# A tuned attention kernel: the last unit gets an order of its own, and GpSimd prepares two of the closing tiles

## The reference, cut to what matters

```python
xn = _layernorm(x)                                   # x: 8 x 256 x 512
q, k, v = heads of xn @ wq.T, xn @ wk.T, xn @ wv.T   # 32 query heads, 8 key/value heads of 128
q, k = rope(q), rope(k)
scores = (q @ k.T) / sqrt(128) * scale + causal      # scale: 0.5 or 1.5 on some columns
s = softmax(scores) @ v, all heads side by side, @ wo.T
g = silu(lora_mixture(xn))                           # top 2 of 4 experts
out = x + s * g
```

## Time and profile before

| | us |
|---|---|
| median of 3 runs | 1355.3 (1354.82 to 1359.77) |
| the profiled execution, its own time | 1357.92 |
| its span, first to last instruction | 1356.1 |
| PE busy | 1322.2 (98%) |
| DVE busy | 969.6 (72%) |
| ACT busy | 961.8 (71%) |
| POOL busy | 423.0 (31%) |
| granted TensorE clock, mean | 0.99 |

### The profile page before, as it was taken

One profiled execution on the slowest core, in us unless ns is written; L12 is line 12 of the kernel. 1 busy time (PEld: TensorE's weight loads), 2 busy tenths in 40 slices (PEclk: granted clock), 3 DMA queues, 4 the chain that ended last, 5 costly groups with the idle time before them and its releaser, 6 DMA issues.

```text
span 1356.1 us, 22594 instructions
## 1 busy us (share of the span) xinstructions
PE 1322.2 (98%) x6982; PEld 1106.6 (82%) x6982; DVE 969.6 (72%) x2449; ACT 961.8 (71%) x2513; POOL 423.0 (31%) x341
## 2 busy tenths in 40 slices
PE   7599999999999999999999999999999999999997
PEld 5588888788888888888888888888888888888885
DVE  6786678667766777776776777677777767777775
ACT  3586668777777777687776768777676877777773
POOL 4332321403314142143323224141331433223321
PEclk9699999999999999999999999999999999999998
DMA  6000000201100000010000000000000100012223
GB/s 217 16 17 5 24 24 9 62 17 47 47 24 32 0 23 23 0 31 15 23 8 15 15 15 31 0 31 0 23 23 0 31 15 23 8 31 85 73 80 119
DMA packets 23385, 43.64 MB, mean 32 GB/s; under 512 B 2480, under 2 KB 2608, under 8 KB 23344
## 3 DMA queue, kind: packets, MB, share of 16 engines
q1 hardware_dynamic: 20592, 37.76, 9.0%
q10 hardware_dynamic: 2752, 5.38, 1.1%
HBM read 34.74 MB, written 8.39 MB: 32 GB/s over the span
## 4 chain that ended last, share of the span: by engine, by line
PE 93%; DVE 4%; ACT 1%; issue 1%; DMA 1%; POOL 0%; SPq 0%; ACTq 0%; DVEq 0%
PE bank_a L461 19%; PE bank_b L461 18%; PE bank_b L555 13%; PE o_ps L555 12%; PE pv_ps L548 10%; PE pair L532 7%; PE pair L539 6%; PE pair L528 2%; PE pair L530 1%; PE bank_a L518 1%; PE o_ps L461 1%; DVE x_sb L975 1%; PE o_ps L508 1%; DMA x_sb<-x 1%; DVE pT_lo L1117 0%
## 5 line engine op out<-in xcount | busy, mean ns | idle before, releaser
L376 POOL TENSOR_TENSOR rot<-rot,tab 128x512 f32<-128x512 f32 x160 | 208.3, 1304 | 603.2 <-ACT rot L777 602.9
L820 ACT ACTIVATE probs<-probs,row_min 128x128 f32<-128x128 f32 (+1 forms) x512 | 225.5, 447 | 0.0
L839 ACT ACTIVATE pT_hi<-pair 128x768 fp32r<-128x768 f32 x128 | 104.0, 812 | 170.9 <-PE pair L539 170.2
L831 ACT ACTIVATE probs<-probs,row_inv 128x128 f32<-128x128 f32 (+1 forms) x512 | 190.8, 446 | 26.7 <-DVE row_inv L1147 26.4
L1117 DVE TENSOR_TENSOR pT_lo<-pair,pT_hi 128x768 fp32r<-128x768 f32 x128 | 121.7, 950 | 92.6 <-ACT pT_hi L839 92.3
L361 POOL TENSOR_TENSOR w_hi<-raw,zero 128x512 fp32r<-128x512 f32 x74 | 84.8, 1147 | 247.6 <-PE bank_a L461 131.2
L461 PE MATMUL bank_b<-xT_hi,w_hi 128*128 (+1 forms) x380 | 153.3, 403 | 2.8 <-DVE xT_lo L988 2.8
L461 PE MATMUL bank_a<-xT_hi,w_hi 128*128 (+1 forms) x380 | 154.8, 408 | 0.5 <-DVE xT_lo L988 0.4
L1097 DVE TENSOR_TENSOR q_lo<-cosx,q_hi 128x512 fp32r<-128x512 f32 x128 | 118.2, 924 | 47.1 <-ACT q_hi L784 46.9
L461 PE MATMUL bank_b<-xT_hi,w_lo 128*128 (+1 forms) x380 | 149.5, 393 | 0.0
L461 PE MATMUL bank_b<-xT_lo,w_hi 128*128 (+1 forms) x380 | 149.1, 392 | 0.0
(11 more groups left out here) (166 smaller groups left out, 3237.6 us busy)
## 6 DMA issues: line engine op xcount, KB each, us to landing
raw<-w_seq SPq DMA_DIRECT2D x76, 256.0 KB, 2.6
gate_scratch<-b_raw ACTq DMA_DIRECT2D x16, 256.0 KB, 2.0
out<-y_sum SPq DMA_DIRECT2D x16, 256.0 KB, 2.0
x_sb<-x SPq DMA_DIRECT2D x3, 1024.0 KB, 12.6
mid<-x SPq DMA_DIRECT2D x8, 256.0 KB, 2.7
mid<-gate_scratch SPq DMA_DIRECT2D x8, 256.0 KB, 2.9
raw<-x SPq DMA_DIRECT2D x7, 256.0 KB, 2.7
raw<-gate_scratch SPq DMA_DIRECT2D x7, 256.0 KB, 2.9
```

Source lines behind the costliest of these rows:

```text
L376: nc.gpsimd.tensor_tensor(v, v, tab[:, s:s + SEQ].unsqueeze(1).to_broadcast([P, 2, SEQ]), ALU.mult).then_inc(sin_done[kind], 1)
L820: a = nc.scalar.activation(s, s, ACT.Exp, bias=row_min[:, j % 2, i:i + 1], scale=-1.0, accum_out=row_sum[:, i:i + 1])
L831: a = nc.scalar.activation(s, s, ACT.Copy, scale=row_inv[:, i:i + 1])
L839: nc.scalar.activation(pT_hi[:, :, :], pair[j % 2][:, :, 0:ROWS], ACT.Copy).then_inc(pThi_done, 1)
```

## The change

The last unit is written out for itself on PE, ACT and DVE (`pe_closing`, `act_closing`, `dve_closing`). On PE an output tile stands behind each `turn_probs`, where the turned pair is being split. On ACT `low_scores(2)` goes ahead of `normalise_rows(1)`, and `exponents(3)` ahead of `rows_high(2)`. On DVE the tile additions move behind the steps of the items. For tiles 14 and 15 GpSimd first turns `y` into `x + y * gate`. DVE then multiplies the last unit's part by the gate and adds it: two operations after the matmuls in place of three. A fourth place for x and gate, `v_T` and `k_full`, takes tile 14. SP loads tiles 15 and 14 after tile 11, and tiles 12 and 13 after the stores of 10 and 11.

```diff
@@ sp
-            loop(sp, 0, TILES // 2 - 2, two_tiles)
+            loop(sp, 0, TILES // 2 - 3, two_tiles)
             sp.wait_ge(q_ready[H2], UNITS)
             load_xg(TILES - 1, 2)
-            store_tile(TILES - 4)
-            load_xg(TILES - 2, 0)
-            for t in range(TILES - 3, TILES):
+            sp.wait_ge(q_ready[K], UNITS)
+            sp.wait_ge(vt_ps, UNITS)
+            load_xg(TILES - 2, 3)
+            for s in range(2):
+                store_tile(TILES - 6 + s)
+                load_xg(TILES - 4 + s, s)
+            for t in range(TILES - 4, TILES):
                 store_tile(t)
@@ gpsimd
+            def open_tile(t, s):
+                y = y_sum[:, t, :]
+                pool.wait_ge(xg_in[s], 32)
+                pool.wait_ge(y_added, 4 * UNITS - 2 * TILES + t + 1)
+                nc.gpsimd.tensor_tensor(y, y, xg[s][1], ALU.mult).then_inc(base_scaled, 1)
+                pool.wait_ge(base_scaled, t - TILES + 3)
+                nc.gpsimd.tensor_tensor(y, y, xg[s][0], ALU.add).then_inc(base_done, 1)
+            def pool_closing():
+                open_tile(TILES - 2, 3)
+                add_residual(TILES - 4, 0)
+                add_residual(TILES - 3, 1)
+                open_tile(TILES - 1, 2)
@@ tensor
+        def pe_closing():
+            pe = nc.tensor
+            n = 4 * UNITS
+            pe.wait_ge(probs_ready, n - 3)
+            turn_probs(0)
+            output_tile(1, 0, n - 4, n - 7)
+            next_scores(2, n - 3, (), None)
+            pe.wait_ge(v_ready, UNITS)
+            prob_value(0)
+            pe.wait_ge(probs_ready, n - 2)
+            turn_probs(1)
+            output_tile(1, 1, n - 4, n - 6)
+            next_scores(3, n - 2, (), None)
+            pe.wait_ge(attn_ready, n - 3)
+            prob_value(1)
+            pe.wait_ge(probs_ready, n - 1)
+            turn_probs(2)
+            output_tile(0, 0, n - 2, n - 5, weights=KV_HEADS)
+            pe.wait_ge(pT_ready, n - 1)
+            prob_value(2)
+            pe.wait_ge(probs_ready, n)
+            turn_probs(3)
+            output_tile(0, 1, n - 2, n - 4)
+            pe.wait_ge(attn_ready, n - 1)
+            output_heads(1, 0, pair[0][:, 0, :], range(0, 2))
+            pe.wait_ge(pT_ready, n)
+            prob_value(3)
+            output_heads(1, 1, pair[0][:, 1, :], range(0, 2))
+            pe.wait_ge(attn_ready, n)
+            for t in range(2):
+                output_heads(1, t, pair[0][:, t, :], range(2, GROUP)).then_inc(o_done, 1)
@@ scalar
+        def act_closing():
+            rows_high(0, 125, 124)
+            low_scores(2, 127)
+            normalise_rows(1, 126)
+            rows_high(1, 126, 125)
+            attn_high(0, 125, 122)
+            exponents(2, 127)
+            low_scores(3, 128)
+            normalise_rows(2, 127)
+            attn_high(1, 126, 122)
+            exponents(3, 128)
+            rows_high(2, 127, 126)
+            normalise_rows(3, 128)
+            rows_high(3, 128, 127)
+            attn_high(2, 127, 124)
+            attn_high(3, 128, 124)
@@ vector
+        def close_tile(t, done, s):
+            dve, i = nc.vector, t - TILES + 2
+            dve.wait_ge(base_done, i + 1)
+            dve.wait_ge(o_done, done)
+            nc.vector.tensor_tensor(xg[s][1], pair[0][:, i, :], xg[s][1], ALU.mult).then_inc(o_gated, 1)
+            dve.wait_ge(o_gated, i + 1)
+            dve.wait_ge(y_final, t)
+            nc.vector.tensor_tensor(y_sum[:, t, :], y_sum[:, t, :], xg[s][1], ALU.add).then_inc(y_final, 1)
+        def dve_closing():
+            rows_low(0, 125)
+            mask_rows(2, 127)
+            rows_low(1, 126)
+            add_tile(10, 123, final=10, bank=o_ps[:, :], xg_set=0)
+            attn_low(0, 125)
+            row_inverse(127)
+            mask_rows(3, 128)
+            attn_low(1, 126)
+            add_tile(11, 124, final=11, bank=bank_b[:, :], xg_set=1)
+            row_inverse(128)
+            rows_low(2, 127)
+            add_tile(12, 125, final=12, bank=o_ps[:, :], xg_set=0)
+            rows_low(3, 128)
+            attn_low(2, 127)
+            add_tile(13, 126, final=13, bank=bank_b[:, :], xg_set=1)
+            attn_low(3, 128)
+            close_tile(14, 127, 3)
+            close_tile(15, 128, 2)
```

## The result

The changed kernel takes 1350.98 us (median of 6 runs) against 1356.72 for the kernel before in the same runs: ratio 0.9959, 95% interval 0.9946 to 0.9973. One of its six executions was a slow one (2181.95 us, mean granted clock 0.557), and the ratio goes by the other five, 1350.82 to 1351.34. The kernel is faster by 0.41%. The prediction took anything within 0.5% for "same", to which it gave 0.60, and the time lies inside its range of 1346.5 to 1352.0. The profiled execution took 1350.96, its span is 1349.0.

What follows compares the result with a forecast made beforehand. TensorE, busy 98% of the span, was taken as the bound, so its waits and slow clock near the end and the VectorE close count. The laid-out queues gave 6.8 off 1355.3, less 0.2: 1348.7, range 1346.5 to 1352.0.

Steps and rivals of the forecast that it cites:

- Step 1: ScalarE's normalise_rows(1) now stands behind low_scores(2), so turn_probs(1) starts at 1323.2 after a new TensorE wait of 0.8.
- Step 2: Tile 11 runs while the turned pair 1 is split, so the 1.89 wait before scores(3) is gone.
- Step 3: prob_value(1) follows scores(3) to 1328.9; the attn_low(0) it needs ends on VectorE at 1327.84, just in time.
- Step 4: turn_probs(2) waits 0.8 for normalise_rows(2); tile 12 starts 0.35 late, its attn_low(1) being behind mask_rows(3).
- Step 5: Tile 12 covers the old 2.58 wait before prob_value(2); rows_low(2) ends at 1333.95 with nothing to spare.
- Steps 6 and 7: TensorE's last tiles run to 1345.44, four closing VectorE operations instead of six end at 1346.90; span 1349.3, 6.8 less.
- The 0.2 for leaks: Allowance taken off the 6.8 because steps 3, 5 and 6 have 0 to 0.2 to spare, leaving 6.6.
- GpSimd and DMA: Prepared tile 15 ready 1.4 ahead, loads hidden with 0.5 for tile 13; only tile 12's multiply meets GpSimd, for 0.1 to 0.2.
- clock rival: The old slow clock is part of the gain, or the new queues slow once: gain 5.1 or 5.3, 1350.2 or 1350.0; chance 0.20.
- Close late: GpSimd's tile 15 or the load of 13 comes late, giving 1 to 3 back: 1350 to 1352; chance 0.07.
- Waits only move: Each TensorE wait taken away comes back behind ScalarE: 1 to 2 us and the shorter VectorE end remain, 1352 to 1354; 0.05.
- Slower: The new waits drop TensorE's clock to 0.50 from 1323 to the end: slower by 13, 1368; chance 0.04.

Runs made afterwards that it cites:

- The repeat: The changed kernel run again with no edit: closing stretch (last unit's first turn of probabilities to span's end) 32.97 us, median 1352.22 against 1357.99 for the kernel before.
- Experiment 8: The changed kernel with normalise_rows(1) ahead of low_scores(2) on ScalarE: closing stretch 31.91, ratio 0.9946 to the kernel before.
- Experiment 6: The changed kernel with tile 11's matmuls put back ahead of turn_probs(1): closing stretch 35.06, ratio 0.9968 to the kernel before.
- Experiment 5: The changed kernel with tile 12's matmuls put back behind turn_probs(3): closing stretch 37.76, ratio 0.9995 to the kernel before.
- experiment 3: The changed kernel's orders and loads alone, GpSimd preparing nothing, three closing operations each for tiles 14 and 15: closing stretch 34.29, ratio 0.9964 to the kernel before.
- prepared tiles alone: The last unit in the old order, but tiles 14 and 15 prepared by GpSimd and closed with two operations: closing stretch 38.59, ratio 0.9994 to the kernel before.
- experiment 2: The kernel before with useless matmuls filling its two TensorE waits in the last unit: closing stretch 38.00, ratio 0.9982 to the unfilled kernel.
- experiment 7: The changed kernel with GpSimd's two prepared tiles both after adding x to tiles 12 and 13: closing stretch 34.35, ratio 0.9960 to the kernel before.
- split tiles: The changed kernel with normalise_rows(1) first, tiles 12 and 13 halved, VectorE's additions of tiles 10 and 11 earlier: closing stretch 31.97, ratio 0.9942 to the kernel before.

## Why the prediction was right

- **What bounds it, and the sum.** 6.8 was worked out for the closing stretch, 6.62 measured. The repeat is 6.55 under the same profile of before.
- **Step 1**, new wait of 0.8 before `turn_probs(1)`: measured 0.80. Experiment 8 shows that it is paid in full (1.0 with the handover).
- **Step 2**, the 1.89 gone by tile 11's cover: right. Experiment 6 brings it back.
- **Step 3**, just in time: `prob_value(1)` started with no wait listed.
- **Step 4**, 0.8 and 0.35: measured 0.66 and 0.33.
- **Step 5**, the 2.58 gone: right. Experiment 5 shows tile 12 as the cover, which alone is worth 4.9, clock included. "Nothing to spare" held: `prob_value(2)` starts at 1333.48, `rows_low(2)` ends at 1333.42.
- **Steps 6 and 7**: from tile 14's last half (1342.04) to the last VectorE operation's end (1346.59) 4.55 passed, 4.38 were worked out. Four closing operations in place of six are worth 1.39 (experiment 3).
- **The 0.2 for leaks.** 6.8 less 0.2 is 6.6, and 6.62 came, but the 0.2 was taken for steps 3, 5 and 6, and these leaked nothing. Counted from the first turn, TensorE starts every step within 0.07 of the layout, and the last 12 matmuls at 25.94 in both. The 0.18 is lost in step 7. From the start of those 12 matmuls to VectorE's first closing operation the layout has 1.58, as before. The changed kernel took 1.76, in both of its profiles, "order alone" 1.70, "prepared tiles alone" 1.64. So 0.12 comes with the new order: the last 12 matmuls start as `attn_low(3)` ends, and the second follows the first by 0.34, not 0.23. And 0.06 comes with the two-operation close, for which no run shows a reason. The size of the allowance was right, its place was luck. The lines are of the kernel before, of "order alone" and of "prepared tiles alone":

```profile
1347.91 0.39 PE L555 MATMUL pair<-w_hi,attn_hi 128*128 128x512 f32 x1
```
```profile
1343.84 0.50 PE L577 MATMUL pair<-w_hi,attn_hi 128*128 128x512 f32 x1
1345.54 0.69 DVE L1322 TENSOR_TENSOR y_sum<-pair,y_sum 128x512 f32<-128x512 f32 x1 [1.75 <-PE pair L577]
```
```profile
1349.25 0.39 PE L579 MATMUL pair<-w_hi,attn_hi 128*128 128x512 f32 x1
```

- **GpSimd and DMA.** GpSimd was through 1.5 before it was needed, 1.4 forecast. The sign of the one meeting was the wrong way round: tile 12's multiply (1334.36, 0.69) started almost at GpSimd's end, and it was GpSimd's next addition that took 1.64. Both are hidden. I took 4.1 as the slowest landing; with the added loads behind one another it was 5.3, and it did no harm, since the data of `k_full` was there at 1327.7 and wanted at 1333.17, that of `cosx` much later. The loads of 12 and 13 had more room than the 0.5 forecast for tile 13: they landed some 2.1 before their multiplies. The two slowest loads:

```profile
cosx<-gate_scratch SPq DMA_DIRECT2D x1, 256.0 KB, 4.9
...
k_full<-gate_scratch SPq DMA_DIRECT2D x1, 256.0 KB, 5.3
```

- **The clock.** Counted as 1.7 of the gain, 1.5 by experiment 2. That the new waits would leave it at 1.00 held in all windows of the changed kernel from 1316 to 1346.
- **The signs.** Of the three signs of being wrong that were named, two did not come: a clock of 0.50 after 1323, and a wait before `prob_value(2)`. The third did: the stretch before 1316 changed its length. The last unit began 0.48 earlier than in the profile of before, and 0.75 later in the repeat. That sign was badly chosen, since this start moves between executions of one program; the closing stretch leaves it out.
- **The absolute time.** 1348.7 forecast, 1350.98 measured. 1.4 of these 2.3 is the kernel before, whose median was 1355.3 in the runs shown and 1356.72 over all. With 6.6 off that it would be 1350.1, and the rest, 0.9, is inside the interval of the ratio (1349.4 to 1353.1 from 1356.72). The start of the last unit varies by 3.4 between profiles of identical instructions, so a gain of 6.6 does not show sharper than this in a few runs. The time alone would not have carried the forecast. 1350.98 lies above the forecast's own 1347.0 to 1349.6, 0.8 over the clock rival's 1350.2 and among the late close's 1350 to 1352; it is the closing stretch that decides between them. And the repeat's median of 1352.22, with the same gain (0.9951), lies above the range's top of 1352.0. That the first one fell inside was in part luck.
- **The rivals.** "Close late" was made real by experiment 7: it costs 1.45, within its 1 to 3. "The clock gives less" had no case in these profiles: the clock was down in the one of before, and filling the waits gave 1.5. "Waits only move" happened to the small part that steps 1 and 4 say. "Slower" had nothing for it.

That part of the gain depends on where the clock falls in other executions of the kernel before stays open: only one of its executions was traced.

## What to carry to other kernels

Lay out an in-order schedule by hand before trusting a reordering: durations of one trace, 0.04 per handover, one queue per engine. Here nine of ten closing stretches came within 0.35 us of what was expected; the tenth missed by 1.7, because the sum left out a place in VectorE's and ScalarE's queues. Place independent matmuls where a result is being split by other engines, and on those engines put what TensorE asks for next ahead of what it asks for later (one swap of two ScalarE steps was worth 1.0, one of the value split and the pair split 1.4). Let a helper engine's work on SBUF end before the closing that it serves: here that decided over 0.36 and 1.45.

## What the runs showed of the hardware

- Waits of TensorE of 1.89 (before, "prepared tiles alone", "tile 11 back"), 2.58 (the first two of these) and 3.23 us ("tile 12 back") were followed by a stretch at 1.2 GHz. Waits of 0.80, of 0.66 and 0.33 close together, one of 1.10 ("split tiles") and one of 1.34 were not. Useless matmuls in the waits kept the clock at 2.4 GHz (1.00 in the window over both waits).
- A VectorE operation on two SBUF inputs beside a GpSimd operation took 0.77 to 1.67 instead of 0.69 (128x512, all operands float32), ending some 0.55 after GpSimd's end. One with a PSUM input took its 0.69. The other way round GpSimd took 1.59 to 1.65 instead of 1.29. The Trainium skill, SBUF — State Buffer, Who interferes with whom, says that a VectorE instruction with two SBUF inputs contends with a GpSimd instruction that reads SBUF. The rows agree, and what is paid in them is the rest of the other's operation.
- Six loads of 256 KB issued one behind the other landed up to 5.3 us after their issue, against 2.6 to 3.1 where only a pair was sent.
